# A causal attention layer and a two-layer local transformer on one core: tables made inside the first stage, weights waited for in halves, and stages that hand over rows without waiting for the store

## The chip, the cores and the metric

The program runs on one core of a Trainium2 chip. The core has five engines with instruction queues of their own: TensorE (PE in the profile, its weight loads PEld), VectorE (DVE), ScalarE (ACT), GpSimd (POOL) and SyncE (SP), which here only issues DMAs. They meet through semaphores. The metric is the device time of one execution in microseconds (us); the median of several runs is compared.

## What is computed

```python
x = x + attention(x)          # 8 sequences of 512 tokens, 256 channels, 16 heads of 16, causal
x = layernorm(x)
y = x
for l in range(2):            # local transformer, 8 heads of 64, window 128
    h = shift_token(x)        # second half of the channels comes from the token before
    q, k, v = split(h @ wqkv[l]); q, k = rotary(l2norm(q) * qs, l2norm(k) * ks)
    x = x + window_attention(8 * q, k, v) @ wo[l]     # keys at most 128 back
    h = layernorm(shift_token(x)) * lg + lb
    a, g = split(h @ w1[l] + b1[l])
    x = x + (a * gelu(g)) @ w2[l] + b2[l]
out = layernorm(y + x)
```

All arrays are fp32. A matmul is split: each operand is rounded to a high part, the rest is its low part, and three products (high x high, low x high, high x low) are added. So each weight needs a high part (made on ACT) and a low part (DVE: raw minus high) before the first matmul with it.

## The kernel before

The program is a chain of five stages, each a Python function that puts one `nc.Block()` on the five queues: `first_attention`, then for each of the two layers `local_attention` and `feed_forward`. Each stage works through the 8 sequences. Its order is a list `STEPS` written out by hand, with names like `st:12` (scores, transposed, unit 12), `sm` (scores for the maxima), `ms` (causal mask on POOL), `pv` (probabilities by values), `z0` to `z3` (normalise and turn the head outputs), `out` and `end`; steps that begin with `f_` prepare the next sequence. `steps()` runs the `f_` steps of sequence 0, a hardware loop of 7 passes over all steps, and then the steps without `f_` for the last sequence, written out once more. Each queue runs the same list and does its own part of each step.

Before the first stage stand two small blocks. `constants()` (line 67) makes the identity matrices and mask tables on POOL, 15 instructions. The block at line 1613 sets `zero_row` on DVE and stores it to row 0 of the two `after_attn` arrays, and SP waits until both stores have landed. A block ends with a barrier of all five engines.

`first_attention` starts with loads from SP (lines 221 to 230): `xin`, the weights `w_raw` in one DMA, six bias DMAs, eight for `w_out`. All of the weights and biases count on one semaphore, `w_loaded`, and ACT's first instruction waits for all seven (line 348: `act.wait_ge(w_loaded, 112)`), rounds `w_hi` in two halves and `wo_hi`, and only then takes `xt_hi` from the turned input. DVE does `w_lo`, `wo_lo`, `xt_lo` in that order, and PE's first projection (line 475, step `f_qk:0`) waits for `w_lo` and `xt_lo`. POOL meanwhile sets `half`, `tri` and the constant rows of `K` (lines 278 to 290) and later makes `qk_lo` (line 305). Queries and keys go through DRAM (`qk_parts`, lines 240 to 258) to be stacked by head.

The end of `first_attention`: after the last `out` steps POOL makes `rs` (lines 329, 331), then the normalised rows `out` in four instructions (line 336), issues their store (line 339) and waits for it:

```python
                steps(pool, do)
                pool.wait_ge(stored, 16 * NB)
```

The weights of the next stage are loaded into buffers that are free by then (`ahead.load`, lines 645 to 648; raw halves in `qk_hi` and `qk_lo`, `wo` in `part_f`), and split after all steps: `ahead.high` on ACT (lines 656, 657), `ahead.low` on DVE (lines 662, 664). `ahead.first` loads the first sequence of the next stage into `xin`. The other stages end in the same way, with a store on POOL (lines 825 and 1372) and the same wait for it; in `local_attention` the next weights are split inside the last sequence, with only the last parts (lines 1244 to 1251) after it.

## Time and profile before

| | us |
|---|---|
| median of 3 runs | 2063.98 (2062.27 to 2068.06) |
| the profiled execution, its own time | 2061.79 |
| span of its trace, first to last instruction | 2060.3 |
| PE busy | 1815.2 (88%) |
| DVE, ACT, POOL busy | 1141.5, 941.3, 940.9 |
| mean granted TensorE clock | 0.922 |

PE, the busiest engine, is busy 88% of the span. By the trace, the stages start at about 7.6, 564.9, 1068.7, 1292.7 and 1798.6 us. PE's longest idle stretches are not inside the loops but at the program's start (PE's first projection starts at 21.06 us) and at the stage ends: from 548.3 to 565.0 us after the first attention, and some 5 to 6 us at each later one. In the timeline rows a line begins with the start and the duration in us; "x4" is the number of instructions merged in it, and the duration is then that of all of them; the bracket at the end is the idle time of the engine before it and what ended it. "SPq" and "POOLq" are rows of an engine's sequencer: DMA issues, waits, drains and barrier semaphores.

### The profile page before, as it was taken

The numbers are of one execution on the slowest core, as the hardware profiler recorded it, in microseconds if no ns is written. First come the engines' busy times: TensorE is split into PE (matmuls) and PEld (weight loads), VectorE is DVE, ScalarE is ACT, GpSimd is POOL, SyncE is SP. The second block draws the span as 40 slices with busy tenths as digits, with TensorE's granted clock in tenths as the row PEclk, the third lists the DMA queues.
The fourth block names the chain that finished last, engine by engine and source line by source line (L and its number), as shares of the span: only waits on it lengthen the run. The fifth ranks groups of instructions, "written<-read, shape, count | busy, mean of one in ns | idle before, by whom it ended". The sixth has DMA issues, their size and how long they took to land. (4 is left out here: it accounts for less than half of the span.)

```text
span 2060.3 us, 41179 instructions
## 1 busy us (share of the span) xinstructions
PE 1815.2 (88%) x13304; PEld 1348.1 (65%) x13304; DVE 1141.5 (55%) x2885; ACT 941.3 (46%) x1834; POOL 940.9 (46%) x926
## 2 busy tenths in 40 slices
PE   4899988889569999999969999599999999798887
PEld 2556555655346777777758888467777777577676
DVE  3566665656367766766523333766676666333343
ACT  2555555655335554455434444255445555333322
POOL 3355444554435555554433333355554545333433
PEclk8899888987679999999979999799999999889998
DMA  4333343332210000000111112100000000221221
GB/s 124 107 114 102 102 128 106 120 112 62 72 32 12 31 31 31 31 31 20 48 56 41 61 61 92 43 11 31 31 31 31 31 20 4 79 72 51 81 71 41
DMA packets 103655, 121.27 MB, mean 59 GB/s; under 512 B 23290, under 2 KB 75700, under 8 KB 103604
## 3 DMA queue, kind: packets, MB, share of 16 engines
q1 hardware_dynamic: 96692, 95.45, 15.3%
q0 software_dynamic: 6912, 25.17, 3.3%
q8 instruction: 28, 0.46, 0.1%
q14 instruction: 23, 0.19, 0.0%
HBM read 82.55 MB, written 37.77 MB: 58 GB/s over the span
## 5 line engine op out<-in xcount | busy, mean ns | idle before, releaser
L425 DVE TENSOR_REDUCE a_negm<-a_x 128x2 f32<-128x256 f32 (+3 forms) x256 | 202.5, 815 | 142.1 <-PE a_x L539 139.7
L804 POOL TENSOR_TENSOR work<-work 128x512 f32<-128x512 f32 x128 | 164.7, 1286 | 196.8 <-DVE work L953 195.6
L394 ACT ACTIVATE a_PT<-a_c 128x384 f32<-128x384 f32 (+1 forms) x384 | 184.1, 523 | 138.7 <-PE a_c L578 87.3
L971 DVE CUSTOM_DVE_ANT_0 l_x<-l_x,window 128x256 f32<-128x256 f32 (+1 forms) x512 | 184.4, 422 | 44.7 <-PE l_x L1067 44.0
L1462 DVE SCALAR_TENSOR_TENSOR m_hid<-m_a,mw_b,m_gate 128x512 f32<-128x512 f32 x96 | 71.9, 749 | 246.8 <-ACT m_gate L1401 222.7
L1001 PE MATMUL l_f<-w_hi,tails 128*128 128x512 f32 x384 | 174.9, 455 | 15.0 <-DVE work L953 11.9
L1359 POOL TENSOR_TENSOR m_hid_lo<-m_hid,m_hid_hi 128x512 fp32r<-128x512 f32 x80 | 102.8, 1294 | 134.6 <-ACT m_hid_hi L1412 134.4
L882 ACT ACTIVATE l_PT<-l_c 128x512 f32<-128x512 f32 (+1 forms) x256 | 124.7, 539 | 79.0 <-PE l_c L1103 79.0
L1002 PE MATMUL l_f<-w_hi,tails 128*128 128x512 f32 x384 | 155.3, 405 | 0.0
L1003 PE MATMUL l_f<-w_lo,tails 128*128 128x512 f32 x384 | 154.6, 403 | 0.0
L818 POOL TENSOR_TENSOR l_PS<-l_PT 128x768 f32<-128x768 f32 x64 | 119.7, 1871 | 76.0 <-ACT l_PT L882 76.0
L1401 ACT ACTIVATE m_gate<-m_g,mw_b 128x512 f32<-128x512 f32 x80 | 54.7, 684 | 187.0 <-PE m_g L1506 187.0
L533 PE MATMUL a_x<-a_K,a_Q 48*128 48x256 f32 (+2 forms) x512 | 119.6, 435 | 19.3 <-DMA a_K<-qk_parts 17.2
L811 POOL TENSOR_TENSOR work<-work,l_inv 128x512 f32<-128x512 f32 x128 | 131.0, 1045 | 0.0
L822 POOL TENSOR_TENSOR l_zl<-l_zt,l_zh 128x512 fp32r<-128x512 f32 x64 | 82.7, 1302 | 98.5 <-ACT l_zh L888 96.5
L605 PE MATMUL a_f<-a_PT,a_V 128*32 128x512 f32 (+3 forms) x1024 | 101.8, 552 | 26.0 <-POOL a_PT L313 14.6
L313 POOL TENSOR_SCALAR_AFFINE_SELECT a_PT<-a_PT 128x512 f32<-128x512 f32 x128 | 79.7, 648 | 97.3 <-ACT a_PT L394 97.1
L854 ACT ACTIVATE work<-l_f 128x512 f32<-128x512 f32 x128 | 76.5, 598 | 104.0 <-PE l_f L1003 92.8
L1115 PE MATMUL l_o<-l_PT,l_V 128*64 128x256 f32 (+1 forms) x1024 | 112.1, 361 | 11.0 <-ACT l_PT L882 10.1
L1115 PEld LDWEIGHTS l_o<-l_PT,l_V 128*64 128x64 f32 x1024 | 71.7, 137 | 58.8 <-ACT l_PT L882 17.6
L944 DVE TENSOR_REDUCE l_ss<-work 128x8 f32<-128x512 f32 x128 | 87.3, 682 | 39.8 <-ACT work L854 39.7
L1001 PEld LDWEIGHTS l_f<-w_hi,tails 128*128 128x128 f32 x384 | 74.1, 193 | 46.5 <-issue 23.6
(238 smaller groups left out, 5115.6 us busy)
## 6 DMA issues: line engine op xcount, KB each, us to landing
a_Q<-qk_parts SPq DMA_DIRECT2D x192, 64.0 KB, 2.1
a_K<-qk_parts SPq DMA_DIRECT2D x192, 64.0 KB, 2.1
qk_parts<-a_qk_hi SPq DMA_DIRECT2D x32, 256.0 KB, 2.1
qk_parts<-a_qk_lo SPq DMA_DIRECT2D x32, 256.0 KB, 2.1
after_attn<-l_out POOLq DMA_DIRECT2D x16, 512.0 KB, 5.8
xin<-after_attn SPq DMA_DIRECT2D x32, 256.0 KB, 3.1
m_xr<-after_attn SPq DMA_DIRECT2D x16, 512.0 KB, 4.1
xin<-in_L_attn_x SPq DMA_DIRECT2D x8, 512.0 KB, 3.5
```

The costliest lines, as they stand in the source:

```text
L394: nc.scalar.activation(PT[:, p // PG % 2, 2 * (p % PG) + hh, QOFF[t]:QOFF[t] + nq], SC[hh][:, 0:nq], ACT.Exp, scale=AD ** -0.5).then_inc(e ...
L425: dve.tensor_reduce(negm[:, q, 2 * p:2 * p + 2], MX[i % 2][:, :, 0:nk], AX.X, ALU.max, negate=True).then_inc(max_done, 1)
L533: pe.matmul(bank[:, hh, 0:nk], Q[rows, p, P * q:P * q + P], Kk[rows, p, 0:nk], start=True, stop=True)
L804: pool.tensor_tensor(t1[:, par, w, :], t1[:, par, w, :], t2[:, par, w, :], ALU.add)\
L811: pool.tensor_tensor(qk[:, i, w, :].rearrange("p (h d) -> p h d", d=FD), t1[:, par, w, :].rearrange("p (h d) -> p h d", d=FD), inv[:, par, ...
L818: pool.tensor_tensor(PS[:, i % 2], PT[:, i % 2, :, 1:TB, 0:P], PT[:, i % 2, :, 0:TB - 1, P:2 * P], ALU.add).then_inc(ps_done, 1)
L882: nc.scalar.activation(PT[:, p % 2, hh, j:j + 2, :].rearrange("p j q -> p (j q)")[:, 0:nq], SC[hh][:, 0:nq], ACT.Exp, scale=8.0).then_inc( ...
L971: m = dve.tensor_tensor_reduce(out=o, in0=o, in1=mask, scale=-1.0, scalar=-NEG, op0=ALU.add, op1=ALU.min, accum_out=negm[:, q + t, p // 2, ...
L1001: pe.matmul(o, a_hi, r_hi, start=first, stop=False)
L1002: pe.matmul(o, a_lo, r_hi, start=False, stop=False)
L1003: return pe.matmul(o, a_hi, r_lo, start=False, stop=last)
L1115: pe.matmul(OB[rows, P * j:P * j + nq], V[:, j, FD * h:FD * h + FD], PT[:, i % 2, hh, j, 0:nq], start=(j == 0), stop=(j == TB - 1), skip_g ...
```

## The change

It has five parts.

1. The two blocks ahead of the first stage are gone. `make_constants` runs at the head of POOL's queue inside `first_attention`, with the fp32 identity first, and with one table (`window_sw`, four instructions on 64 rows) in place of two others. The zero rows are set by DVE after its other memsets and stored by SP in the last sequence; SP waits for them (`zeros.done`) at the end of the stage.
2. The first weights: `w_raw` is loaded as two DMAs with a semaphore each, the biases in four DMAs with one of their own. ACT takes `xt_hi` first, then each half of `w_hi` when it is there; `wo_hi` moves behind step `f_qe:3` and `wo_lo` into step `f_sm:4`.
3. The weights of the next stage are loaded at the start of the last sequence of the first attention. ACT splits them behind `st:12`, `st:18` and `z3:1`, DVE behind `ms:5`, `z0:2` and `z2:3`.
4. The last sequence's normalised rows are made by DVE (step `end`) instead of by POOL.
5. The stages share one output buffer, `rows_out`, and the semaphore of a stage's stores, `ready`, belongs to the next stage. No stage but the last waits for its stores; the next one waits for `own.ready` before its second load of rows and before it first writes `rows_out`.

```diff
@@ POOL, head of first_attention
+                make_constants(pool, K)
                 pool.memset(half[:, :], -0.5).then_inc(rstd_a, 1)
@@ SP, head of first_attention
-                sp.dma_start(w_raw[:, :, :], w_qkv.rearrange("(k p) n -> p k n", p=P)).then_inc(w_loaded, 16)
-                for m, c in enumerate((0, DM, P, DM + P)):
-                    sp.dma_start(bqk[:, m:m + 1], b_qkv[c:c + P].unsqueeze(1),
-                                 allow_slow_non_contiguous=True).then_inc(w_loaded, 16)
+                for k in range(KT):
+                    sp.dma_start(w_raw[:, k, :], w_qkv[P * k:P * k + P]).then_inc(w_loaded[k], 16)
+                for n in range(2):
+                    sp.dma_start(bqk[:, n::2], b_qkv[DM * n:DM * n + DM].rearrange("(h p) -> p h", p=P),
+                                 allow_slow_non_contiguous=True).then_inc(b_loaded, 16)
@@ ACT, first_attention
-                act.wait_ge(w_loaded, 112)
-                for kt in range(KT):
-                    nc.scalar.activation(w_hi[:, kt, :], w_raw[:, kt, :], ACT.Copy).then_inc(w_split, 1)
-                act.wait_ge(wo_loaded, 128)
-                nc.scalar.activation(wo_hi[:, :, :], wo[:, :, :], ACT.Copy).then_inc(wo_split, 1)
...
                             nc.scalar.activation(xt_hi[:, h, :], FB[h][:, :], ACT.Identity)\
                                 .then_inc(xhi_done, 1)
+                        if isinstance(b, int):
+                            for kt in range(KT):
+                                act.wait_ge(w_loaded[kt], 16)
+                                nc.scalar.activation(w_hi[:, kt, :], w_raw[:, kt, :], ACT.Copy).then_inc(w_split, 1)
+                            act.wait_ge(b_loaded, 64)
@@ where the next weights are split
+        HIGH, LOW = [("st", 12), ("st", 18), ("z3", 1)], [("ms", 5), ("z0", 2), ("z2", 3)]
@@ SP, last sequence of first_attention
+                def tail(name, i):
+                    if (name, i) == FIRST_OF_LAST:
+                        sp.wait_ge(parts_out, NB * 128)
+                        sp.wait_ge(lo_done, NB * 4)
+                        ahead.load(sp, ahead_raw, ahead_wo)
+                        zeros.store(sp)
+                        sp.wait_ge(front_full, NB * NF)
+                        sp.wait_ge(stored, 16)
+                        ahead.first(sp)
+                    elif name == "end":
+                        zeros.done(sp)
@@ POOL, end of first_attention
-                    elif name == "end":
+                    elif name == "end" and not isinstance(b, int):
...
-                pool.wait_ge(stored, 16 * NB)
+
+                pool.wait_ge(out_done, NB * TB)
+                pool.dma_start(dst[NB - 1, 1:1 + S].rearrange("(t p) d -> p t d", p=P), out[:, :, :]).then_inc(stored, 16)
@@ DVE, last sequence of first_attention
+                def tail(name, i):
+                    if (name, i) in LOW:
+                        ahead.low(dve, ahead_raw, ahead_wo, LOW.index((name, i)))
+                    elif name == "end":
+                        dve.wait_ge(rstd_done, NB)
+                        dve.wait_ge(stored, 16 * NB - 16)
+                        for t in range(TB):
+                            dve.tensor_scalar(out[:, t, :], y[:, t, :], mv[:, t, 0:1], rs[:, t:t + 1],
+                                              ALU.subtract, ALU.mult).then_inc(out_done, 1)
@@ local_attention (and so in feed_forward)
+                            sp.wait_ge(own.ready, 16 * NB)
                             sp.dma_start(xin[:, :, :], x[b].rearrange("(t p) d -> p t d", p=P)).then_inc(x_in, 16)
...
-                pool.wait_ge(stored, 16 * NB)
```

The change also moves instructions against each other. The first place is ACT's queue at the start of the program (`a_PT` holds the raw weights there, `a_f` the turned input in PSUM). Before:

```order
L351 ACT_TABLE_LOAD
L351 ACTIVATE w_hi<-a_PT 128x768 [waits a_w_loaded]
L351 ACTIVATE w_hi<-a_PT 128x768
L353 ACTIVATE a_wo_hi<-a_PT 128x1024 [waits a_wo_loaded]
L359 ACTIVATE a_xt_hi<-a_f 128x512 [waits a_front_full] x2
L365 ACTIVATE a_qk_hi<-a_f,a_bqk 128x512 [waits a_parts_out,a_front_full]
L369 ACTIVATE a_part_f<-a_f,a_bqk 128x512 [waits a_lo_done]
```

and now:

```order
L388 ACT_TABLE_LOAD
L388 ACTIVATE a_xt_hi<-a_f 128x512 [waits a_front_full] x2
L393 ACTIVATE w_hi<-a_PT 128x768 [waits a_w_loaded0]
L393 ACTIVATE w_hi<-a_PT 128x768 [waits a_w_loaded1]
L399 ACTIVATE a_qk_hi<-a_f,a_bqk 128x512 [waits a_parts_out,a_front_full,a_b_loaded]
L403 ACTIVATE a_part_f<-a_f,a_bqk 128x512 [waits a_lo_done]
```

The input's two halves stand ahead of the weights, each half of the weights has its own wait, and `wo_hi` is no longer ahead of the first projection's result (`a_qk_hi`).

The second place is DVE's queue in the last sequence of the first attention, steps `z0:2` to `z2:3` and `out:0` (`a_ot` and `a_zn` are head outputs, `a_ztf` the turned ones, `a_y` the rows before normalisation). Before:

```order
L434 RECIPROCAL a_rc<-a_ot 128x16 [waits a_o_free]
L438 TENSOR_TENSOR a_zn<-a_ot,a_rc 128x256 [waits a_z_turned,a_norm]
L432 STREAM_TRANSPOSE a_ot<-a_f 128x512 [waits a_o_full,a_norm]
L434 RECIPROCAL a_rc<-a_ot 128x16 [waits a_o_free]
L451 STREAM_TRANSPOSE a_ztf<-a_on 128x512 [waits a_z_done,a_zn_split]
L438 TENSOR_TENSOR a_zn<-a_ot,a_rc 128x256 [waits a_z_turned,a_norm]
L444 CAST a_on<-a_zn 128x16x16 [waits a_norm]
L446 TENSOR_TENSOR a_on<-a_zn,a_on 128x16x16 [waits a_zn_split]
L451 STREAM_TRANSPOSE a_ztf<-a_on 128x512 [waits a_z_done,a_zn_split]
L458 TENSOR_TENSOR a_y<-a_f,a_xr 128x256 [waits a_y_full,a_out_done,a_xb_ready]
L461 BN_STATS a_st<-a_y 128x6 [waits a_y_done]
```

and now:

```order
L478 RECIPROCAL a_rc<-a_ot 128x16 [waits a_o_free]
L721 TENSOR_TENSOR w_lo<-a_qk_lo,w_hi 128x1536 [waits lw0_hi_done]
L482 TENSOR_TENSOR a_zn<-a_ot,a_rc 128x256 [waits a_z_turned,a_norm]
L476 STREAM_TRANSPOSE a_ot<-a_f 128x512 [waits a_o_full,a_norm]
L478 RECIPROCAL a_rc<-a_ot 128x16 [waits a_o_free]
L495 STREAM_TRANSPOSE a_ztf<-a_on 128x512 [waits a_z_done,a_zn_split]
L482 TENSOR_TENSOR a_zn<-a_ot,a_rc 128x256 [waits a_z_turned,a_norm]
L488 CAST a_on<-a_zn 128x16x16 [waits a_norm]
L490 TENSOR_TENSOR a_on<-a_zn,a_on 128x16x16 [waits a_zn_split]
L495 STREAM_TRANSPOSE a_ztf<-a_on 128x512 [waits a_z_done,a_zn_split]
L723 TENSOR_TENSOR wo_lo<-a_part_f,wo_hi 128x1024 [waits lw0_hi_done]
L502 TENSOR_TENSOR a_y<-a_f,a_xr 128x256 [waits a_y_full,a_out_done,a_xb_ready]
```

The second half of the next stage's `w_lo` stands between the reciprocal and the product of step 2, and `wo_lo` behind the last transpose; before, all three stood behind the variances.

The third place is the end of POOL's queue in the same stage. Before:

```order
L299 TENSOR_TENSOR a_xr<-a_xr,a_bo 128x1024 [waits a_w_loaded,a_xr_in]
L329 TENSOR_SCALAR a_ve<-a_mv 128x4 [waits a_var_done]
L331 TENSOR_TENSOR a_rs<-a_ve,a_half 128x4 [waits a_rstd_a]
L336 TENSOR_SCALAR a_out<-a_y,a_mv,a_rs 128x256 [waits a_stored,a_rstd_done]
L336 TENSOR_SCALAR a_out<-a_y,a_mv,a_rs 128x256 x3
L339 DMA after_first<-a_out 128x4x256 [waits a_out_done]
L218 UNCONDITIONAL_BRANCH [waits a_stored]
```

and now:

```order
L332 TENSOR_TENSOR a_xr<-a_xr,a_bo 128x1024 [waits a_b_loaded,a_xr_in]
L363 TENSOR_SCALAR a_ve<-a_mv 128x4 [waits a_var_done]
L365 TENSOR_TENSOR a_rs<-a_ve,a_half 128x4 [waits a_rstd_a]
L379 DMA after_first<-rows_out 128x4x256 [waits a_out_done]
L243 UNCONDITIONAL_BRANCH
```

The four normalising instructions have left POOL's queue, and no wait for the store stands behind its issue.

## Rows read from the trace of the kernel before

**Rows 1.** Five loop passes: busy PE, PEld, DVE, ACT, POOL, granted clock, DMA share, GB/s.

```profile
185.60:487.00 301.40, 270.18 (x2388) 172.03 (x2387) 186.89 (x313) 164.71 (x343) 148.63 (x178) 0.87 0.37 111
```

**Rows 2.** Timeline of all engines from the start to PE's first projection.

```profile
1.03 0.20 POOL L86 MEMSET ident<- 128x128 f32 x1 [0.29 <-POOLq L1654]
...
4.30 0.28 POOL L106 TENSOR_SCALAR_AFFINE_SELECT window_t<-window_t 128x128 bf16<-128x128 bf16 x1
...
7.63 0.43 SPq L221 DMA_DIRECT2D xin<-in_L_attn_x  x1
...
9.35 7.07 POOL L290 MEMSET a_K<- 32x4096 f32 x2
...
11.18 1.97 PE L493 MATMUL a_f<-ident,xin 128*128 128x128 f32 x8 [11.18 <-DMA xin<-in_L_attn_x]
...
14.90 1.58 ACT L351 ACTIVATE w_hi<-a_PT 128x768 fp32r<-128x768 f32 x2 [5.98 <-DMA a_bo<-in_L_attn_b_out]
16.51 1.83 DVE L410 TENSOR_TENSOR w_lo<-a_PT,w_hi 128x768 fp32r<-128x768 f32 x2 [5.32 <-ACT w_hi L351]
...
21.06 0.77 PE L475 MATMUL a_f<-a_xt_hi,w_hi 128*128 128x512 f32 x1 [7.92 <-DVE a_xt_lo L419]
```

**Rows 3.** Timeline of POOL and SP behind the first projections.

```profile
25.41 1.27 POOL L305 TENSOR_TENSOR a_qk_lo<-a_part_f,a_qk_hi 128x512 fp32r<-128x512 f32 x1 [8.99 <-issue]
...
28.77 0.33 SPq L242 DMA_DIRECT2D qk_parts<-a_qk_lo  x1
...
51.80 2.52 SPq L265 DMA_DIRECT2D a_Q<-a_mrow  x4
```

**Rows 4.** Timeline of ACT in the last sequence: exponentials, then the next weights.

```profile
513.27 1.08 ACT L394 ACTIVATE a_PT<-a_c 128x384 f32<-128x384 f32 x2
...
524.92 0.98 ACT L394 ACTIVATE a_PT<-a_c 128x384 f32<-128x384 f32 x2 [0.29 <-PE a_c L578]
...
541.36 1.47 ACT L656 ACTIVATE w_hi<-a_qk_hi 128x1536 fp32r<-128x1536 f32 x1
```

**Rows 5.** Timeline of DVE, the same sequence and behind it.

```profile
536.28 0.42 DVE L438 TENSOR_TENSOR a_zn<-a_ot,a_rc 128x256 f32<-128x256 f32 x1
...
544.40 0.42 DVE L458 TENSOR_TENSOR a_y<-a_f,a_xr 128x256 f32<-128x256 f32 x1 [3.62 <-POOL a_xr L299]
...
549.39 1.72 DVE L662 TENSOR_TENSOR w_lo<-a_qk_hi,w_hi 128x1536 fp32r<-128x1536 f32 x1
```

**Rows 6.** Timeline of POOL and PE from the last variances to the next stage.

```profile
549.57 1.64 POOL L329 TENSOR_SCALAR a_ve<-a_mv 128x4 f32<-128x4 f32 x1 [5.20 <-DVE a_mv L465]
...
553.80 4.84 POOL L336 TENSOR_SCALAR a_out<-a_y,a_mv,a_rs 128x256 f32<-128x256 f32 x4
558.94 0.86 POOL L339 DMA_DIRECT2D after_first<-a_out  x1 [0.30 <-POOL a_out L336]
...
564.99 1.94 PE L1023 MATMUL l_f<-ident,xin 128*128 128x128 f32 x8 [16.71 <-PEq L630]
```

**Rows 7.** By line, L218 and L331: duration ns min/median/max, first and last start.

```profile
L218 SPq DRAIN  x1: 122/122/122, 521.8 to 521.8; - x1
...
L218 POOLq DRAIN  x1: 1372/1372/1372, 562.6 to 562.6; - x1
...
L331 POOL TENSOR_TENSOR a_rs<-a_ve,a_half x8: 1046/1046/2402, 127.3 to 551.3; 128x4 f32<-128x4 f32 x8
```

**Rows 8.** Timeline of DVE at the last stage's end.

```profile
2054.02 1.38 DVE L1493 TENSOR_SCALAR m_out<-m_y,m_mv,m_rs 128x256 f32<-128x256 f32 x4 [1.48 <-POOL m_rs L1369]
```

**Rows 9.** Both local attentions' ends: the store's issue, the block's drains by line.

```profile
1064.41 0.79 POOL L825 DMA_DIRECT2D after_attn<-l_out  x1 [8.38 <-DVE l_out L986]
...
L760 DVEq DRAIN  x2: 2670/2670/2670, 1063.7 to 1793.4; - x2
...
L760 POOLq DRAIN  x2: 703/711/719, 1067.8 to 1797.7; - x2
```

**Rows 10.** Timeline of DVE at the first feed-forward's end.

```profile
1291.18 1.22 DVE L664 TENSOR_TENSOR wo_lo<-m_ahead_wo,wo_hi 128x1024 fp32r<-128x1024 f32 x1
```

203 lines of the change are left out of this document (112 added, 91 removed).

## The prediction, made before the changed kernel ran

> **What bounds the kernel now.** I read the busy time by stretch first. In the loops PE sets the pace: over five passes of the first attention it is busy 270.2 of 301.4 us [rows 1]. The change leaves every pass of every loop as it is, but for one more wait on a semaphore that has long been reached. So I looked at what stands between the loops: the timeline of the start [rows 2, 3], that of the last sequence of the first attention [rows 4, 5], and the ends of the stages [rows 6 to 10]. The reader is to see there that PE does nothing useful for 21 us at the start [rows 2] and for 16.7 us at the first stage end [rows 6], and which engine ends each of these waits. There the time of a chain goes straight into the span.
>
> **The start.** The loads begin at 7.63 us, behind two blocks [rows 2]. POOL's first table instruction stands at 1.03, behind a barrier that all queues share [rows 2]; SP waits for nothing else in the new order, so its first DMA goes out at about 1.05, 6.6 us earlier. The input lands 3.55 us after its issue (7.63 to 11.18) [rows 2]: 4.6. The turning takes PE 1.97 us: 6.6. The identity is the first table, two instructions of at most 0.3 us each behind 1.03 (0.28 for such a select [rows 2]), and is no limit. Before, ACT waited until 14.90 for the last bias, did both `w_hi` (1.58), waited for `w_out`, and only then took the input. Now it takes the second `xt_hi` at 6.6; I take 0.6 us for it, from 0.79 for a half of `w_hi` with 768 columns against 512. Then `w_hi` runs from 7.15 to 8.7. Weights and biases were there 7.27 us after the first issue (7.63 to 14.90) [rows 2], so at 8.3 at the latest, and only the projection's result at some 14 us needs the biases. DVE follows with `w_lo`, 1.83 us for both and 0.9 behind ACT's last: 9.8. PE starts `f_qk:0` at 9.95 instead of 21.06: **11.1 us**.
>
> Who is late next? POOL. Its queue now holds 15 to 16 table instructions, which ended at 4.6 before and, with a few more waits, end at about 5.9 now; then `half` and `tri`, 1.7 us (from the barrier at 7.63 to 9.35), and the 7.07 us of `K` rows [rows 2]: done at 14.8. The first `qk_lo` started at 25.41 [rows 3], and is due 11.1 earlier, at 14.3. It comes 0.5 us late, but the second, issued from SP at 28.77 and so made from some 27.45, is due at 16.35 while POOL is free at 16.1 (1.27 each [rows 3]). What starts the long series of SP's loads is the landing of the second `qk_lo`, issued at 28.77 [rows 3]. So 0 of the delay gets through. The bound on the other side: POOL's `ve` and `pow` were stretched while DVE ran a subtraction of two SBUF operands, 2.40 us against 1.05 [rows 5 to 7]. If DVE's 1.83 us of `w_lo` held up the setting of `K` in the same way, POOL would be free at 16.6 + 1.3 and the second `qk_lo` 1.6 late. No row has a POOL memset beside such a DVE operation; both rows of a hold-up are of POOL instructions that read SBUF. I take 0 and keep 1.6 for the range. The Trainium skill (SBUF — State Buffer, Who interferes with whom) says that a DVE instruction with two SBUF inputs contends with a GpSimd instruction that reads SBUF and not with one that only writes it. By that rule the memset goes on and the start is worth its 11.1 us; by a lock on all of POOL's work it would be 9.5. The stretched `ve` and `pow` agree with the rule, and no row tests its second half.
>
> `wo_hi` lies in an idle stretch of ACT. `wo_lo` (about 1.2, [rows 10] has one of the same shape) goes ahead of the fifth reduction of `f_sm`, which PE waits for; it delays the first maxima by 0.6 to 1.2. Their four DMAs went out at 51.80, when SP had finished other loads [rows 3], over a microsecond after they were ready. SP's series covers it: 0; without that cover it would cost up to 1.2.
>
> **The next weights, inside the last sequence.** This is the price of the change. ACT's exponentials are a chain with PE there: two score banks, and the next scores wait for the last exponential. Behind `st:12` ACT had no idle time at all (513.27 has none ahead of it), so 1.37 us of `w_hi` (1.47 less the overlap of 0.1) [rows 4] delay the next ones by 1.25; `mt:3` and `pv:1` stand behind these scores on PE. Behind `st:18` ACT idled 0.29 [rows 4]: 1.0 more. `wo_hi` behind `z3:1` finds ACT idle: 0. On DVE, `w_lo` behind `ms:5` finds it idle: 0. But `w_lo` behind `z0:2` (1.72, pipelined some 1.6) [rows 5] stands ahead of `zn` (536.28), which POOL's split, the last transposes, the reload of `xr` on POOL and so the sum at 544.40 all wait for: 1.6. `wo_lo` behind `z2:3` lies in the 3.62 us for which DVE waited for POOL's `xr`: 0. The SP loads move from the end to the start of the sequence, ahead of two groups of small row loads; the stretch has some 15 us for them. Together **-3.85 us**; the ends are 0, if the chain has more slack than I see, and 5.5, if DVE's and POOL's reads of SBUF also meet.
>
> **The end of the first attention.** From the start of `ve` to PE's first instruction of the next stage it is 564.99 - 549.57 = 15.4 us [rows 6]. In this stood `ve` and `pow` beside DVE's subtractions, four instructions of together 4.84, the store and the wait for its landing, a drain from 562.6 on of 1.37 [rows 7] and a second barrier. Now `ve` and `pow` run undisturbed: at the last stage's end, in the same pattern, DVE waited 1.48 for both [rows 8], so 1.4 from the start of `ve`. DVE's four normalising instructions take 1.38 [rows 8], POOL's wait for them 0.3 and the issue of the store 0.86 [rows 6]: 3.95. Then a drain, which I take at its 1.37 with 0.15 ahead of it, and the 1.0 us from its end (563.97) to the next stage as before: 6.5. **15.4 - 6.5 = 8.9 us**; with a drain of 0.71, as at the other ends [rows 9], 9.6.
>
> **The other ends.** After each local attention POOL waited for the landing and drained until 1068.5 and 1798.4 [rows 9]. DVE drained until 1066.4 and 1796.1, since its last weights are split there [rows 9]. POOL alone would now be through at 1064.41 + 0.79 + 0.15 + 0.72 = 1066.1. So DVE is last, and the gain is not the whole wait: **2.1 + 2.3 us**. After the first feed-forward DVE's `wo_lo` ends at 1292.40 [rows 10], 0.3 before the next stage; the wait for the store is hidden there already, and its removal gives 0. The last stage keeps its wait. The new waits for `ready` stand on SP and DVE behind waits for PE that come tens of us later, while the store is down within 2.8 us of its issue (559.8 to the drain at 562.6): 0.
>
> **Sum.** 11.1 - 3.85 + 8.9 + 2.1 + 2.3 = 20.6 us. The span goes from 2060.3 to 2039.7, the profiled execution's own time from 2061.8 to 2041.2; the median of the runs before is 2.2 us above that execution, so 2063.98 - 20.6 = 2043.4, rounded 2043.
>
> **The rivals.**
> - **The drain waits for the store.** Before, no drain of POOL was issued with a store of its own in flight, so no row shows it. If it holds until the landing, at most 2.8 us after the issue's end, and then takes its time as before, both local ends give 0 and the first one 2.8 less: 13.4 us, 2050.6. For it: the drains took 0.7 and 1.37 even with nothing in flight. Against it: SP's drain at the end of the first attention takes 0.12 us at 521.8, while the load issued just ahead of it is under way [rows 7]. Chance 0.14.
> - **The insertions cost nothing**, because the pacing is not that of ACT and DVE there: 24.5 us, 2039.5. The idle gaps of 0.29 speak against it. Chance 0.13.
> - **POOL or a landing is late at the start**, by 1.6 to 3 us: 2045 to 2046.5. For the landings speaks that all loads now go out within 3 us of each other and of the table load; against it, that they stood as close before. Chance 0.08.
> - **Slower: PE's clock.** The granted clock in the first attention's loop is 0.87 [rows 1], a mean between its levels of 1.2 and 2.4 GHz. One hundredth of it costs 0.62 us a pass (54 us busy per pass) and 4.3 us over seven. All passes now start at other moments; if the mean in this loop fell by 0.05, to 0.82, the loss would eat the gain of 20.6, below 0.81 the kernel is slower by more than 0.3%, and at 0.78 it would take 2082. Nothing in a pass changes, which speaks against it. Chance 0.03.
>
> **How the numbers follow.** The forecast, all terms near their size, has 0.62, with a range of its own of 2040 to 2047. The range of 2038 to 2051 takes in the first three rivals. A difference of 0.3%, 6.2 us, is about what a measurement of this kernel can tell from no change. Faster by more than that is below 2057.8: all cases but the clock and a heap of small misses, 0.93. Within it 0.04, slower 0.03.
>
> **What would show it right or wrong.** In the new profile: SP's first DMA at 1.05 and the first projection at 9.95; POOL's `K` memsets of 3.5 us each or longer; the first `a_Q` load from DRAM at 19.7 (30.8 before); the last sequence 3.9 us longer; `ve` far below its 1.64 us; 6.5 us from there to the next stage; DVE's drain as the last of each local end, and POOL's drain there no longer than 0.7 us. A first projection after 12 us, a POOL drain of 2 us or more, or a loop pass that differs from 60.3 us would make the prediction wrong.

## The result, and the profile after

| | kernel before | changed kernel |
| --- | --- | --- |
| median of six runs (us) | 2063.00 (2062.24 to 2068.06) | 2048.25 (2043.63 to 2052.87) |
| profiled execution (us), its span | 2061.79, 2060.3 | 2043.63, 2042.2 |
| mean granted clock of the profiled execution | 0.922 | 0.924 |

The ratio is 0.9925, with a 95% interval of 0.9906 to 0.9945: some 15 us faster by the medians, against 20.6 forecast. In a second comparison, of five runs with nine of the kernel before, it was 0.9924 (0.9911 to 0.9938), with medians of 2047.30 and 2063.99. The profiled execution fell by 18.2 us, its span by 18.1, and it was the fastest of its six. So there are two questions: which term of the forecast's 20.6 us was too large, and why the runs of the changed kernel lie 9 us apart.

A table of places, each the first instruction of its kind, shows where the time went:

| place | before | after | shift |
| --- | --- | --- | --- |
| PE, first projection | 21.06 | 9.77 | -11.29 |
| PE, turning for the next sequence, first loop pass | 67.09 | 55.99 | -11.10 |
| DVE, aggregates ahead of the last sequence | 495.01 | 483.03 | -11.98 |
| DVE, first sum with `xr` in the last sequence | 544.40 | 536.21 | -8.19 |
| DVE, the last aggregates | 549.11 | 539.70 | -9.41 |
| PE, first local attention | 564.99 | 548.41 | -16.58 |
| PE, first feed-forward | 1068.95 | 1053.19 | -15.76 |
| PE, second local attention | 1292.73 | 1276.15 | -16.58 |
| PE, second feed-forward | 1798.85 | 1781.03 | -17.82 |
| DVE, last aggregates of all | 2052.18 | 2034.08 | -18.10 |

The start, which answers to [rows 2, 3]. The rows are of the timeline of the changed kernel: start, busy time, engine, line, operation, and in brackets the idle time before with what ended it.

```profile
1.04 0.44 SPq L246 DMA_DIRECT2D xin<-in_L_attn_x  x1
...
7.02 1.56 ACT L393 ACTIVATE w_hi<-a_PT 128x768 fp32r<-128x768 f32 x2
7.88 1.83 DVE L459 TENSOR_TENSOR w_lo<-a_PT,w_hi 128x768 fp32r<-128x768 f32 x2
9.77 0.80 PE L528 MATMUL a_f<-a_xt_hi,w_hi 128*128 128x512 f32 x1 [3.28 <-DVE w_lo L459]
...
14.40 1.27 POOL L338 TENSOR_TENSOR a_qk_lo<-a_part_f,a_qk_hi 128x512 fp32r<-128x512 f32 x1
...
19.50 0.81 SPq L284 DMA_DIRECT2D a_Q<-qk_parts  x2
```

POOL's fills of `K`, from two shorter windows of the same timeline, which list them one by one:

```profile
7.25 3.50 POOL L323 MEMSET a_K<- 32x4096 f32 x1
...
10.81 3.51 POOL L323 MEMSET a_K<- 32x4096 f32 x1
```

PE's first projection waits for DVE's `w_lo`, at 9.77 where 9.95 was forecast, and the first load of `a_Q` goes out at 19.50 where it was 19.7. POOL's two fills of `K` take 3.50 and 3.51 us. The first of them lies wholly over DVE's 1.83 us of `w_lo`, the second beside no such work, and they are equally long. The hold-up of 1.6 us that the forecast kept for its range is not there.

The last sequence, which answers to [rows 4, 5], from the timeline of all engines:

```profile
511.18 2.87 POOL L346 TENSOR_SCALAR_AFFINE_SELECT a_PT<-a_PT 128x512 f32<-128x512 f32 x2 [6.27 <-ACT a_PT L431]
511.36 2.19 DVE L721 TENSOR_TENSOR w_lo<-a_qk_hi,w_hi 128x1536 fp32r<-128x1536 f32 x1
...
515.15 1.23 POOL L346 TENSOR_SCALAR_AFFINE_SELECT a_PT<-a_PT 128x512 f32<-128x512 f32 x2
...
520.06 2.60 POOL L346 TENSOR_SCALAR_AFFINE_SELECT a_PT<-a_PT 128x512 f32<-128x512 f32 x4 [3.67 <-ACT a_PT L431]
...
526.32 1.70 DVE L721 TENSOR_TENSOR w_lo<-a_qk_lo,w_hi 128x1536 fp32r<-128x1536 f32 x1
527.93 0.41 DVE L482 TENSOR_TENSOR a_zn<-a_ot,a_rc 128x256 f32<-128x256 f32 x1
...
536.21 0.42 DVE L502 TENSOR_TENSOR a_y<-a_f,a_xr 128x256 f32<-128x256 f32 x1 [2.68 <-POOL a_xr L332]
```

The second `w_lo` stands ahead of `zn`, as forecast. The first was costed at nothing, because DVE idles there. It meets POOL's masks: the pair at 511.18 takes 2.87 us where the next pair takes 1.23, and DVE's own instruction takes 2.19 us where the other takes 1.70. Nothing of this reaches PE: ahead of the masks at 520.06 POOL is idle for 3.67 us, waiting for ACT's exponentials, and the delay of 1.6 us is lost in that idle time. The stretching itself is what the Trainium skill states (SBUF — State Buffer, Who interferes with whom) of a DVE instruction with two SBUF inputs beside a GpSimd instruction that reads SBUF; the trace agrees, and the fills above agree with what the page says of GpSimd instructions that only write SBUF.

The end of the first attention, which answers to [rows 6, 7], from the timeline:

```profile
540.16 0.23 POOL L363 TENSOR_SCALAR a_ve<-a_mv 128x4 f32<-128x4 f32 x1 [3.98 <-DVE a_mv L509]
540.47 1.05 POOL L365 TENSOR_TENSOR a_rs<-a_ve,a_half 128x4 f32<-128x4 f32 x1
541.55 1.38 DVE L519 TENSOR_SCALAR rows_out<-a_y,a_mv,a_rs 128x256 f32<-128x256 f32 x4 [1.50 <-POOL a_rs L365]
543.24 0.84 POOL L379 DMA_DIRECT2D after_first<-rows_out  x1 [1.72 <-DVE rows_out L519]
...
548.41 0.88 PE L1084 MATMUL l_f<-ident,xin 128*128 128x128 f32 x3 [9.56 <-PEq L686]
```

The drains of that block, by line (duration in ns min/median/max, first and last start):

```profile
L243 DVEq DRAIN  x1: 1420/1420/1420, 541.6 to 541.6; - x1
L243 POOLq DRAIN  x1: 4158/4158/4158, 543.2 to 543.2; - x1
```

The store in the view of the DMAs (size, median us from issue to landing):

```profile
after_first<-rows_out POOLq DMA_DIRECT2D x1, 512.0 KB, 3.4
```

The first local attention's end, which answers to [rows 9], from the timeline:

```profile
1048.99 0.79 POOL L886 DMA_DIRECT2D after_attn<-rows_out  x1 [8.84 <-DVE rows_out L1047]
...
1053.19 0.56 PE L1589 MATMUL m_w<-mw_bet,work 128*128 128x1 f32 x2 [4.97 <-PEq L819]
```

The drains of both local attentions' ends:

```profile
L819 DVEq DRAIN  x2: 2670/2670/2670, 1048.3 to 1776.1; - x2
L819 POOLq DRAIN  x2: 3773/3784/3796, 1049.0 to 1776.8; - x2
```

DVE's drain ends at 1051.0, POOL's at 1052.76, 0.38 us behind the landing of its store at 1052.38: POOL is still the last. In all seven traces in which POOL issues its last stores without waiting for them, its drain ends 0.71 us behind the landing at the first attention's end and 0.38 us at the local ends and the first feed-forward's. From the store's issue to PE's next instruction it is 4.20 us, and was 1068.95 - 1064.41 = 4.54. The gain is 0.34 us where 2.1 was forecast, and at the second local attention 0.5 (4.19 against 4.70) where 2.3 was.

### The profile page after: what moved, and what is told of

It reads as the page before. It is cut to its first block and busy times, and to the rows that moved or that the text cites. A ratio compares the mean times of both kernels' runs of the same rounds, so it can differ in the third digit from the quotient of the medians.

```text
span 2042.2 us, 41246 instructions
## 1 busy us (share of the span) xinstructions
PE 1815.5 (89%) x13304; PEld 1346.9 (66%) x13304; DVE 1143.1 (56%) x2889; ACT 940.6 (46%) x1834; POOL 935.2 (46%) x922
## 5 line engine op out<-in xcount | busy, mean ns | idle before, releaser
L589 PE MATMUL a_x<-a_K,a_Q 48*128 48x256 f32 (+2 forms) x512 | 118.2, 432 | 18.1 <-DMA a_K<-qk_parts 15.4
```

Source lines behind the costliest of these rows:

```text
L589: pe.matmul(bank[:, hh, 0:nk], Q[rows, p, P * q:P * q + P], Kk[rows, p, 0:nk], start=True, stop=True)
```

## The experiments

Each kernel was compared with the kernel before on the same chip. Its median stands beside the ratio with its interval. The changed kernel's own is 2047.30 (0.9924, 0.9911 to 0.9938) in the second comparison. The experiments ran on three chips, so two of them are set side by side by their ratios rather than by their medians; where the intervals overlap, only the traces tell them apart.

### Which wait stands at the stage ends: the store's queue, the wait

The last stores from SP (shown for the first attention; the two local attentions and the first feed-forward in the same way). POOL's stores and SP's count on separate semaphores, and the waits of the next stage are for both.

```diff
                 steps(sp, do, tail)
+                sp.wait_ge(out_done, NB * TB)
+                sp.dma_start(dst[NB - 1, 1:1 + S].rearrange("(t p) d -> p t d", p=P), out[:, :, :]).then_inc(ahead.down, 16)
...
                 steps(pool, do)
-
-                pool.wait_ge(out_done, NB * TB)
-                pool.dma_start(dst[NB - 1, 1:1 + S].rearrange("(t p) d -> p t d", p=P), out[:, :, :]).then_inc(stored, 16)
```

> Base is the changed kernel (profiled execution 2043.6 us). The last store of the first attention, of both local attentions and of the first feed-forward is issued from SP instead of POOL; all other stores stay. Theory 1 (a POOL drain holds until POOL's own store has landed: in the trace of the changed kernel POOL's drain stands from 543.21 to 547.37 and the store lands at 546.66, at the local ends from 1048.96 to 1052.76 with the landing at 1052.38; SP's drain does not wait): the first attention's end then waits for DVE's drain (until 542.99) and SP's issue, about 543.6, and the next stage starts 3.8 us earlier; both local ends wait for DVE's drain (until 1050.95), 1.8 us earlier each; the end of the first feed-forward gives nothing, since DVE splits until 1275.82. Together 7.4 us less than the changed kernel: a profile of some 2036. Theory 2 (every engine's drain waits for the transfers that it issued itself): the same as the changed kernel within 1 us. Theory 3 (the drain is long for another reason and stays long on POOL without a store): also no gain.

Measured: 2040.97 us (2038.62 to 2044.29), ratio 0.9881 (0.9866 to 0.9897), faster than the changed kernel beyond both intervals. The timeline of this kernel at the first attention's end:

```profile
541.77 1.38 DVE L518 TENSOR_SCALAR rows_out<-a_y,a_mv,a_rs 128x256 f32<-128x256 f32 x4 [1.49 <-POOL a_rs L367]
543.22 0.40 SPq L308 DMA_DIRECT2D after_first<-rows_out  x1
...
544.83 1.09 PE L1088 MATMUL l_f<-ident,xin 128*128 128x128 f32 x4 [5.76 <-PEq L685]
```

Its drains there:

```profile
L243 POOLq DRAIN  x1: 2406/2406/2406, 540.6 to 540.6; - x1
L243 DVEq DRAIN  x1: 1418/1418/1418, 541.8 to 541.8; - x1
L243 SPq DRAIN  x1: 114/114/114, 543.7 to 543.7; - x1
```

SP's drain takes 0.11 us just behind the issue of a 512 KB store. From the last aggregates to the next stage it is 4.92 us, against 8.71 in the changed kernel: 3.8 us, the number of theory 1. At the first local end it is 3.15 us from DVE's last sum (1044.23) to PE (1047.38), against 4.93 (1048.26 to 1053.19): 1.8, as expected. Theory 2 falls with SP's drain of 0.11 us, theory 3 because POOL's drain, with no store in flight, ends at 543.05 and ahead of DVE's. The profile as a whole came out at 2041.4 and not at 2036, for a reason that belongs to the third group of experiments: six of its passes in the second local attention are 0.9 us longer. All these stores have the same size and land 3.4 us after their issue, so the runs do not tell the landing itself from another step of the same store that ends then.

The wait put back (shown for the first attention; the local attentions and the first feed-forward in the same way):

```diff
                 pool.dma_start(dst[NB - 1, 1:1 + S].rearrange("(t p) d -> p t d", p=P), out[:, :, :]).then_inc(stored, 16)
+                pool.wait_ge(stored, 16 * NB)
```

> Base is the changed kernel. The one edit: POOL waits again for its last store at the end of the first attention, of the local attentions and of the first feed-forward. Theory 1 (the drain waits for the landing anyway): only what the drain still costs behind the wait is paid: 0.3 us at each local end (issue of the store to PE's next instruction 4.54 us before, 4.20 now), up to 0.9 at the first end, 0 at the feed-forward's: 1 to 1.5 us slower than the changed kernel. The forecast's own step (a drain of 0.7 to 1.37 us that does not wait): 2.8 + 2.1 + 2.3 = 7.2 us slower.

Measured: 2050.10 us (2047.38 to 2050.59), ratio 0.9920 (0.9906 to 0.9934): not to be told from the changed kernel, where the forecast's step would have made it 7 us slower. From the timeline and from the view of that block's line:

```profile
546.68 0.84 POOL L379 DMA_DIRECT2D after_first<-rows_out  x1 [1.72 <-DVE rows_out L519]
```

```profile
L243 POOLq DRAIN  x1: 1377/1377/1377, 550.3 to 550.3; - x1
```

With the wait, the drain starts 0.2 us behind the landing (550.11) and takes 1.38 us. Without it, the drain covers the landing and ends 0.7 us behind it. From the store's issue to PE's next instruction it is 6.05 us with the wait (552.73 - 546.68) and 5.17 without: 0.9 us at this end and, in the same way, 0.5 and 0.8 us at the local ones is all that the removed waits give, where the forecast had 7.2 us for the three. The ratio puts the kernel 0.8 us behind the changed one, well within the intervals.

### The splits in the last sequence, the normalising, the start

The splits behind the sequence again, on ACT and on DVE:

```diff
-        HIGH, LOW = [("st", 12), ("st", 18), ("z3", 1)], [("ms", 5), ("z0", 2), ("z2", 3)]
+        HIGH, LOW = [], []
...
                 steps(act, do, tail)
+                act.wait_ge(front_full, NB * NF)
+                for n in range(KT + 1):
+                    ahead.high(act, ahead_raw, ahead_wo, n)
...
                 steps(dve, do, tail)
+                for n in range(KT + 1):
+                    ahead.low(dve, ahead_raw, ahead_wo, n)
```

> Base is the changed kernel. The splits of the next weights stand behind the whole last sequence again, on ACT and on DVE (there behind the four normalising instructions); their loads stay where the change put them. Theory 1 (the splits inside cost 3.8 us up to the sum with xr, by the shifts -11.98 at the start of the last sequence and -8.19 at its first sum): the sum comes 3.8 us earlier, of which 1.2 may go again to the clock, as they came back in the changed kernel. ACT's three instructions fit into its idle time. DVE's three, together 4.5 us, start at about 539 + 1.4 and end near 544, while POOL's drain waits for the landing until about 544.5: hidden. So 2.5 to 3.8 us faster than the changed kernel. Theory 2 (the insertions cost nothing, the shift is the clock's alone): the same, or up to 1 us slower where DVE's splits end after POOL's drain.

Measured: 2048.14 us (2043.79 to 2050.01), ratio 0.9910 (0.9896 to 0.9924). The ratio is 0.0014 below the changed kernel's, 2.9 us and within the expected 2.5 to 3.8, but the intervals overlap, so the runs alone cannot tell the two apart. In the trace the shift against the changed kernel goes from +5.35 at the start of the last sequence to +1.81 at its last aggregates: 3.5 us come back in this stretch. The stretch can be followed place by place. In the changed kernel the exponentials behind ACT's first `w_hi` come 1.1 to 1.2 us later than with the splits behind, those behind the second another 1.0, and `zn` behind DVE's second `w_lo` another 1.5. POOL's work behind the stretched masks comes 1.5 us later and the next masks not at all. The rest goes with PE's clock, and nearly cancels: the product with `V` behind the first `w_hi` takes 0.6 us less (3.7 against 4.3, at a granted clock of 0.63 against 0.54), and the first half of the next one, which DVE waits for, 0.5 us more (at 0.50 against 0.59). Behind that, +1.89 at PE's next stage: DVE's splits are hidden by POOL's drain. So the part of the change that was meant to clear the stage's end costs its 3.5 us in full and, for as long as POOL's drain stands there, buys nothing.

The normalising back on POOL:

```diff
-                    elif name == "end":
-                        dve.wait_ge(rstd_done, NB)
-                        dve.wait_ge(stored, 16 * NB - 16)
-                        for t in range(TB):
-                            dve.tensor_scalar(out[:, t, :], y[:, t, :], mv[:, t, 0:1], rs[:, t:t + 1],
-                                              ALU.subtract, ALU.mult).then_inc(out_done, 1)
...
                 steps(pool, do)
+                pool.wait_ge(rstd_done, NB)
+                pool.wait_ge(stored, 16 * NB - 16)
+                for t in range(TB):
+                    pool.tensor_scalar(out[:, t, :], y[:, t, :], mv[:, t, 0:1], rs[:, t:t + 1],
+                                       ALU.subtract, ALU.mult).then_inc(out_done, 1)
```

> Base is the changed kernel. POOL normalises the last rows of the first attention again, in four instructions (4.84 us together before), behind ve and pow; DVE does nothing there. Theory: 4.84 + 0.3 against 1.4 + 0.3 us, so the next stage starts 3.4 us later against the last aggregates; POOL's drain still waits for the landing. Rival: DVE's drain (1.4 us in the changed kernel) is gone from the chain and makes up for a part: 2.5 us later.

Measured: 2053.09 us (2048.76 to 2056.85), ratio 0.9948 (0.9933 to 0.9964).

```profile
543.22 4.85 POOL L380 TENSOR_SCALAR rows_out<-a_y,a_mv,a_rs 128x256 f32<-128x256 f32 x4
548.36 0.86 POOL L383 DMA_DIRECT2D after_first<-rows_out  x1 [0.30 <-POOL rows_out L380]
```

From the last aggregates (541.29) to the next stage (553.57) it is 12.28 us against 8.71: 3.6 us, as the theory has it. This is half of the 7.2 us that the first end gained.

The two halves of the start. The tables in a block of their own, with the zero rows in a second (the three places in the first attention where the same calls go are not shown):

```diff
...
         zeros = ZeroRows(nc, ctx, after_attn)
+        with nc.Block() as block:
+            @block.gpsimd
+            def _(pool):
+                make_constants(pool, K)
+        with nc.Block() as block:
+            @block.vector
+            def _(dve):
+                zeros.set(dve)
+
+            @block.sync
+            def _(sp):
+                zeros.store(sp)
+                zeros.done(sp)
```

> Base is the changed kernel. The tables stand in a block of their own again and the zero rows in a second one, both ahead of the first attention; everything else, the order of the first sequence and its waits for halves of the weights too, stays. Theory: the two blocks are worth what SP's first DMA moves by: it went out at 7.63 in the kernel before, at 1.04 in the changed one; with the table instructions of the change, which end 0.9 later, it goes out at about 8.5. So 7.5 us slower than the changed kernel, and the other 3.6 of the start's 11.1 us are the new order of ACT's first sequence. Rival: POOL's K rows, done at 14.32, are what bounds the start, and with the blocks back they move by the whole 7.5 too, or less, if the tables in their own block are no longer ahead of them: 5 to 6 us slower.

Measured: 2056.08 us (2054.77 to 2060.11), ratio 0.9960 (0.9946 to 0.9974). SP's first DMA goes out at 8.51, PE's turning starts 7.43 us later than in the changed kernel and the second turning 7.34: 7.5 was expected, and the ratios lie 7.4 us apart.

All of ACT's splits ahead of its first sequence (the places in the steps where the same lines go are not shown):

```diff
...
+                act.wait_ge(b_loaded, 64)
+                for kt in range(KT):
+                    act.wait_ge(w_loaded[kt], 16)
+                    nc.scalar.activation(w_hi[:, kt, :], w_raw[:, kt, :], ACT.Copy).then_inc(w_split, 1)
+                act.wait_ge(wo_loaded, 128)
+                nc.scalar.activation(wo_hi[:, :, :], wo[:, :, :], ACT.Copy).then_inc(wo_split, 1)
+
                 def do(name, i, b):
```

> Base is the changed kernel. ACT waits for all biases and for w_out ahead of its first sequence and splits all the first attention's weights there, as before; the loads still go out at 1.04 us and in the new order, the tables stay on POOL's queue. Theory (the other part of the start's 11.1 us): before, the first projection came 13.4 us behind the first load (7.63 to 21.06); with two DMAs fewer ahead of w_out it comes at 13.5 to 14.5 instead of 9.8, so the first load of a_Q is 3.7 to 4.7 us later. Rival (POOL's K rows, done at 14.3, bound the start): only the part beyond POOL counts, and the first load of a_Q is 3 us later at most.

Measured: 2052.80 us (2052.50 to 2053.58), ratio 0.9942 (0.9927 to 0.9957). The first projection comes at 15.67 and the first load of `a_Q` at 25.91, 6.4 us later than in the changed kernel. Both sizes that I expected are too small. ACT takes the input only at 11.96 (5.67 in the changed kernel), behind the last bias (8.87) and `w_out` (10.88), and DVE's `w_lo` stands behind its `xt_lo` in the changed order, so both follow one after the other. The halves don't add up, and the order in which one counts them matters: blocks first 21.06 to 15.67 = 5.4 and then the order of ACT 5.9, or the order of ACT first 21.06 to 17.19 (from the trace with the tables in blocks) = 3.9 and then the blocks 7.4. Either way 11.3. Of the 6.4 us the ratios show 3.7 (0.9942 against 0.9924), with intervals that overlap and are too wide to settle it; in the trace PE's first local attention comes 7.9 us later than in the changed kernel's.

### Why the runs lie 9 us apart: a lock, or the clock

The changed kernel once more, unchanged:

> The changed kernel unchanged, for the spread of its runs and as the base of this comparison on the same chip. Theory 1 (lock in the second local attention) and theory 2 (clock in the first attention) both give runs from 2042 to 2053; under theory 1 the trace has passes of the second local attention of 57.7 and of 58.7 us wherever it is longer than 2042.2, under theory 2 the difference lies within the first 490 us, where the granted clock is lower.

Measured: 2047.30 us (2045.35 to 2049.35). Its trace has a span of 2043.8 us, 1.6 above the first one's: one pass of the second local attention lasts 58.6 us there, the others from the second pass on 57.7, and the first loop pass of the first attention 59.5 instead of 59.3. Both theories have a part in it, and neither is refuted. Two places differ between executions of the same instructions. The rows are of stretches of one pass each: from and to, length, busy time of PE, PEld, DVE, ACT and POOL with their instructions, granted clock, DMA share, GB/s. First the first loop pass of the first attention, in the changed kernel, in the one with the splits behind (same instructions in this stretch) and in the one without the clamp of the local attentions (`ln_bias`, further down; same instructions here again):

```profile
55.99:115.27 59.28, 54.88 (x489) 34.37 (x489) 36.50 (x58) 33.09 (x69) 25.14 (x30) 0.88 0.37 108
```

```profile
56.56:120.39 63.83, 59.85 (x488) 38.00 (x488) 37.16 (x58) 33.30 (x69) 24.00 (x30) 0.79 0.34 101
```

```profile
56.59:121.68 65.09, 61.18 (x488) 38.59 (x489) 37.15 (x58) 33.45 (x69) 24.50 (x30) 0.76 0.32 99
```

The pass takes up to 5.8 us more, and PE's busy time grows by 6.3 us as the granted clock falls from 0.88 to 0.76: more of the stretch at 1.2 GHz. That is theory 2, and it holds for this pass. Why the clock comes out so in one execution and not in another, no trace shows.

Then one pass of the second local attention, in the changed kernel, in the one with the stores from SP and in the one without the clamp:

```profile
1385.49:1443.21 57.72, 55.95 (x442) 41.72 (x441) 38.87 (x118) 29.68 (x60) 31.19 (x25) 1.00 0.08 27
```

```profile
1378.92:1437.55 58.63, 56.22 (x443) 41.67 (x442) 39.41 (x118) 29.57 (x60) 31.12 (x25) 1.00 0.08 27
```

```profile
1388.22:1445.85 57.63, 55.86 (x443) 41.62 (x442) 37.15 (x114) 30.18 (x60) 31.21 (x25) 1.00 0.08 27
```

Here the clock is full in all three, and still the second pass is 0.9 us longer. The instruction that differs is DVE's small clamp. The timeline around it, changed kernel first, then the one with the stores from SP:

```profile
1407.89 0.18 DVE L1009 TENSOR_SCALAR l_ss<-l_ss 128x16 f32<-128x16 f32 x1
1407.91 1.30 POOL L865 TENSOR_TENSOR work<-work 128x512 f32<-128x512 f32 x1
```

```profile
1401.32 1.32 DVE L1012 TENSOR_SCALAR l_ss<-l_ss 128x16 f32<-128x16 f32 x1
1401.33 1.29 POOL L868 TENSOR_TENSOR work<-work 128x512 f32<-128x512 f32 x1
```

An instruction of 0.18 us takes 1.32 us, exactly until POOL's product has ended. The expectation further down puts POOL ahead in the second pair; the rows show both within 0.01 us. In the second local attentions of ten traces the two instructions start within 0.05 us of each other 87 times. POOL was 11 ns or more behind in 67 of them, and 64 of these clamps took 0.18 us. It was at most 4 ns behind, or ahead, in the other 20, and 17 of these took 1.32 us or more. So which engine comes first by a hundredth of a microsecond goes with 0.9 us of a pass; the three exceptions on either side are not explained. The Trainium skill (SBUF — State Buffer, Who interferes with whom) says that `tensor_scalar` can take the pair of ports that DVE shares with GpSimd, and that "Whoever issues first gets the shared pair for the whole instruction"; the traces agree in 81 of the 87 pairs, with 0.18 against 1.32 us.

The clamp taken out of DVE, for the test and as an improvement (the memset of `tiny` on POOL and the waits for it are not shown):

```diff
...
-                        act.wait_ge(ss_done, n + 1)
+                        act.wait_ge(ss_raw, 2 * n + 2)
...
-                        nc.scalar.activation(inv[:, par, :], ss[:, par, :], ACT.Ln).then_inc(log_done, 1)
+                        nc.scalar.activation(inv[:, par, :], ss[:, par, :], ACT.Ln, bias=tiny[:, :]).then_inc(log_done, 1)
...
-                        if w == 1:
-                            dve.wait_ge(ss_raw, b * 8 + i + 1)
-                            dve.tensor_scalar(ss[:, par, :], ss[:, par, :], 1e-24, None, ALU.max)\
-                                .then_inc(ss_done, 1)
```

`tiny` holds 1e-24. In place of the larger of the sum of squares and 1e-24 the logarithm takes their sum; the two differ in effect only where the sum of squares is not far above that size.

> Base is the changed kernel. In the local attentions DVE's small TENSOR_SCALAR that clamps the sums of squares (128x16, in place in SBUF) is gone; ACT's logarithm adds 1e-24 as its bias instead. Theory 1 (a lock between DVE and POOL in SBUF decides the length of a pass: in the changed kernel's trace this instruction takes 0.18 us in the third block of a pass when it starts 0.02 us ahead of POOL's `work` product, in the trace with the last stores from SP it takes 1.33 us when POOL is 0.01 us ahead, and that pass is 0.94 us longer, 58.66 against 57.72): all passes of the second local attention last 57.7 us or less in every execution, and less also because the 0.77 to 0.85 us of the fourth block go: 0 to 7 us faster than the changed kernel, and a smaller spread of the runs (9.2 us between the six runs of the changed kernel). Theory 2 (the spread is the granted clock of PE in the first attention, whose first full pass lasted 59.3, 62.4 and 63.8 us in three traces with the same instructions): the spread stays above 6 us and the second local attention's passes still come in two lengths.

Measured: 2042.07 us (2041.80 to 2046.34), ratio 0.9896 (0.9881 to 0.9911), 5.2 us below the changed kernel on the same chip. All passes of the second local attention but the first last 57.6 us (the first 58.1, in the changed kernel 58.2). Three of the four runs lie within 0.3 us; the fourth is the profiled one, with the first pass of 65.09 us at a clock of 0.76. So neither theory has the spread alone: without the clamp the median falls by several us and most of the scatter is gone, while the clock still gives single runs that are some 4 us longer. That the whole fall of the median is the lock is not shown. In the ten traces with the clamp, 17 passes of the second local attention have a clamp of 1.32 us or more and are some 0.9 us longer: 1.6 us per execution. Six passes with no such clamp last 346.8 us in the changed kernel and 346.3 without any clamp, which gives 0.5 us more. That is some 2 us in an execution like the traced ones. The fall of 4.3 to 5.2 us in the medians would need four or five long passes in the typical execution. Two of the ten traces have that many (six and four), and the executions that were not profiled have no trace.

The same edit on the kernel before:

> Base is the kernel before, with the one edit of ln_bias: DVE's small clamp is gone, ACT's logarithm adds 1e-24 as its bias. What it tells: whether the kernel before loses time to the lock between DVE and POOL as the changed one does. Theory 1 (before, the order of the two engines fell right nearly always: its own trace has all seven passes of the second local attention at 57.7 us): 0 to 2 us faster than the kernel before, and ln_bias, 2042.1 us in the median, stands 20 us below it. Theory 2 (before loses as often as after): 4 to 6 us faster, as ln_bias was against the changed kernel, and the change is worth some 17 us with or without the lock.

Measured: 2059.97 us (2057.97 to 2061.49), ratio 0.9978 (0.9967 to 0.9988): 4.3 us below the kernel before. The interval of the ratio is 2.5 to 6.8 us, which speaks for theory 2: the seven good passes in the trace of before were then this one execution's luck, though no trace of that kernel shows a long one. Without the clamp the change is worth 2059.97 - 2042.07 = 17.9 us by the medians of two chips and 16.9 by the ratios, with it 16.7 (2063.99 - 2047.30) or 14.8 (2063.00 - 2048.25).

### A version that beats both

On the stores from SP, the splits are placed by the idle times that the traces show (in the first attention, the local attentions and the first feed-forward):

```diff
-        HIGH, LOW = [("st", 12), ("st", 18), ("z3", 1)], [("ms", 5), ("z0", 2), ("z2", 3)]
+        HIGH, LOW = [("st", 10), ("st", 15), ("z3", 1)], [("z2", 0), ("z2", 1), ("z2", 3)]
...
                     if (name, i) in LOW:
+                        if (name, i) == LOW[1]:
+                            dve.wait_ge(masked, 4 * AG * NB)
...
                     if name == "zn" and i >= 2:
                         ahead.low(dve, i - 2)
-                    elif name == "out":
-                        ahead.low(dve, KT)
+                        if i == 3:
+                            ahead.low(dve, KT)
...
                     elif name == "y":
+                        if ahead is not None and isinstance(b, int):
+                            ahead.low(dve, [ahead_raw[:, k, :] for k in range(KT)], ahead_wo[:, :, :], 0)
...
-                    for n in range(KT + 1):
+                    for n in range(1, KT + 1):
```

> Base is the changed kernel with the last stores issued from SP. In the last sequence of the first attention the splits stand where both engines idle: ACT's w_hi behind st:10 (6.0 us idle) and st:15 (2.9 us idle), DVE's w_lo behind z2:0 (4.3 us idle) and behind z2:1 once POOL has masked its last tiles (4.1 us idle). DVE splits the feed-forward's last weights ahead of the output rows (4.2 us idle) and the first of the next attention's ahead of the first feed-forward's rows. Theory (the order of engines at the stage ends, as the drains show them): 3.8 us less in the last sequence, of which up to 1.2 can go to the clock; both local ends then end with SP's issue instead of DVE's 2.6 us of splits, 1.8 us less each; the first feed-forward's end 1.7 us less. With the 7.4 us of the stores from SP about 15 us less than the changed kernel: a profile of 2028 to 2031, if the passes keep their length. Rival (DVE's splits meet POOL's reads of SBUF in the new places too): each of the places gives back up to 1.5 us, 2034.

Measured: 2026.67 us (2025.84 to 2030.51), ratio 0.9828 (0.9814 to 0.9841), the profiled execution 2025.84, 2 us below the expected band. Against the changed kernel the last sequence is 3.6 us shorter. The first local end, from the timeline:

```profile
1043.05 0.42 DVE L1053 TENSOR_TENSOR rows_out<-l_s,l_xr 128x256 f32<-128x256 f32 x1 [1.02 <-PE l_s L1070]
1043.50 0.38 SPq L850 DMA_DIRECT2D after_attn<-rows_out  x1
...
1044.48 1.69 PE L1603 MATMUL m_w<-mw_bet,work 128*128 128x1 f32 x14 [1.47 <-PEq L820]
```

From DVE's last sum to PE it is 1.43 us, against 4.93 in the changed kernel. The first feed-forward's end comes 1.7 us earlier, as expected. The rival falls: in the first attention DVE's three splits take 1.72, 1.76 and 1.18 us and met no POOL instruction that reads SBUF.

With the clamp out as well:

> The kernel best1 with the clamp moved into the logarithm's bias as in ln_bias. Theory 1 (lock): as best1, less 0 to 7 us that single executions lose in the second local attention, with the smallest spread of all: a median of 2025 to 2029. Theory 2 (clock): as best1, with its spread.

Measured: 2021.77 us (2019.74 to 2024.17), ratio 0.9794 (0.9781 to 0.9808): 42 us below the kernel before and 25 below the changed one. It is lower than expected by 3 us. Taking the clamp out is again worth 4.9 us in the median; that this is the lock is not shown, since the one trace of the kernel with the clamp has no long pass in the second local attention.

## Why the prediction was right or wrong

The time of 2043 was too low by 5 us, though the range of 2038 to 2051 held it. It left the forecast's own range (2040 to 2047) and came near the first rival's 2050.6. The direction and the places were right. By the prediction's own sign, a POOL drain of 2 us or more, its account of the stage ends was wrong. That the profiled execution came within 2.4 us of its forecast (2043.6 against 2041.2) is in part luck: the terms below give 16.6 us, 1.2 of it from a stretch that the forecast had not priced, and this was the fastest of six executions.

- **The start, 11.1: right.** 11.10 us at the first loop pass. The times of the loads, of PE, ACT and DVE are within 0.2 us; POOL's are 0.4 and 0.5 us early (tables done at 5.5 where 5.9 was said, `K` at 14.3 where 14.8 was). That POOL is the next one late, and that nothing of it gets through, held too. By a lock on all of POOL's work it would have been 9.5; the fills of `K` at 3.50 and 3.51 us decide for the rule.
- **The splits inside, -3.85: right, and in its parts.** From -11.98 to -8.19 it is 3.8 us at the first sum with `xr`, and 3.5 against the trace with the splits behind. There the three terms are 1.1 to 1.2 (1.25 forecast), 1.0 (1.0) and 1.5 (1.6). The step "On DVE, `w_lo` behind `ms:5` finds it idle: 0" has the right price, but not for the reason given: idle DVE is not enough, since POOL was reading then and its masks were stretched by 1.6 us. It cost nothing because POOL had an idle stretch of 3.67 us behind it, which the forecast had not looked for.
- **Up to the last aggregates, 1.2 us came back.** PE's granted clock was 0.59 from 541 to 549 us before and 0.76 in the matching 6.7 us after. That was not foreseen. From the first sum to the last aggregates it is 4.71 and 4.66 us in the two traces with the old order, and 3.46 to 3.54 in all eleven with the change, also in that with the splits behind. So it comes with the change, but not with where the splits stand, and the runs do not show with which part.
- **The first end, 8.9: 7.2.** The normalising on DVE and the undisturbed `ve` and `pow` are worth what was said. The step that failed is "Then a drain, which I take at its 1.37". The drain waits for POOL's own store. The rival had this mechanism with a price of 2.8 us. It is 1.7: the landing came 2.6 us after the issue's end, and the drain ended 0.7 us behind it instead of 0.15 + 1.37.
- **The local ends, 2.1 + 2.3: 0.3 and 0.5.** "POOL alone would now be through at ... 1066.1" is the same failed step. DVE was not last, POOL was.
- **The weight of the rival, 0.14: too low.** Against it stood SP's drain of 0.12 us [rows 7]. The runs confirm that row (0.11 us behind SP's own store). But it was a row of another engine, whose transfers the profile lists under another kind of queue (hardware_dynamic, POOL's software_dynamic). A row on the same engine did not exist, and then the two cases should have been about as likely.
- **The waits for `ready`, the first feed-forward's end, `wo_lo`: 0, right.** At the feed-forward's end DVE's splits are last, as said.
- **The clock, and the length of a pass.** The rival asked for the mean over seven passes. What the traces show is single passes: the first loop pass lasts from 59.3 to 65.1 us with the same instructions. The price of 0.62 us for a hundredth of the clock was somewhat high; between these two it is 5.8 / 12 = 0.5. The 60.3 us of a pass are a misreading: the stretch of [rows 1] holds 2388 PE instructions and a pass 489 to 493, so it is 4.9 passes and not five. The full passes last 59.1 to 62.1 us in the trace of before, and as a sign of being wrong this number was of no use.
- **The rest.** The terms give 11.1 - 2.6 + 7.2 + 0.9 = 16.6. The way to the profile's 18.1 are passes that lie a microsecond better or worse, at the end of the first attention's loop (-11.10 to -11.98) and in the second local attention's last pass and around it (-16.20 to -17.82, of which the end explains 0.5). From that profile to the medians it is 3.7 to 4.6 us, where the forecast had taken over the 2.2 of the kernel before.
- **Missed altogether: the near tie in the local attentions.** The kernel before has the clamp too, so it takes little from the gain (16.9 to 17.9 without it, 14.8 to 16.7 with it). It makes a single profiled execution a poor measure of a median: the changed kernel's profile was 3.7 to 4.6 us below its medians, that of before 1 to 4 us.
